# Projection and causal attention of layer 2 in one program

## What is computed

```python
h = rmsnorm(layernorm(x), ln1_w)
qkv = einsum('bsh,oh->bso', h, wqkv)     # 384 columns
q, k, v = 16 heads, 4 heads, 4 heads of 16 columns
q, k = apply_rope(q, cos, sin), apply_rope(k, cos, sin)
k, v = repeat(k, 4), repeat(v, 4)
scores = einsum('bqhd,bkhd->bhqk', q, k) * 16**-0.5   # causal mask
attn = einsum('bhqk,bkhd->bqhd', softmax(scores), v)
x = x + attn @ wo.T                       # then a mixture of experts
```

## Time and profile before

| | us |
|---|---|
| median of 3 runs | 2072.73 (2072.46 to 2073.15) |
| the profiled execution, its own time | 2073.89 |
| span of its trace | 2072.1 |
| PE busy | 1817.0 (88%) |
| DVE busy | 1227.2 (59%) |
| ACT busy | 990.4 (48%) |
| POOL busy | 504.0 (24%) |

### The profile page before, as it was taken

How to read it: one execution, slowest core, us unless ns; L and a number is a source line. 1 busy time by engine, 2 the same in 40 slices (tenths; PEclk the granted TensorE clock), 3 DMA queues, 4 the chain that set the end, 5 groups by cost and what they waited for, 6 DMA issues and landing times. The chain is left out here.

```text
span 2072.1 us, 33460 instructions
## 1 busy us (share of the span) xinstructions
PE 1817.0 (88%) x10357; PEld 958.4 (46%) x10358; DVE 1227.2 (59%) x3167; ACT 990.4 (48%) x2129; POOL 504.0 (24%) x740
## 2 busy tenths in 40 slices
PE   5795779884899999999999999999875799999994
PEld 5622656552333333333333333332665466666662
DVE  2388236886888888787888888782466122222220
ACT  2201115431477776767777776867643122222221
POOL 2100302366302030210203030000387122333331
PEclk9997899985899999999999999999986899999997
DMA  4000000000000000000000000000356222222223
GB/s 134 0 0 0 1 1 1 4 18 0 1 2 2 1 2 2 2 1 2 2 2 2 2 2 2 2 1 1 114 170 220 57 47 47 47 47 47 45 47 97
DMA packets 55929, 60.83 MB, mean 29 GB/s; under 512 B 11533, under 2 KB 51638, under 8 KB 55734
## 3 DMA queue, kind: packets, MB, share of 16 engines
q1 hardware_dynamic: 33712, 33.86, 5.5%
q0 software_dynamic: 13440, 18.36, 5.2%
q10 hardware_dynamic: 8646, 6.96, 1.0%
HBM read 34.82 MB, written 28.12 MB: 30 GB/s over the span
## 5 line engine op out<-in xcount | busy, mean ns | idle before, releaser
L1452 ACT ACTIVATE prob<-pS 128x512 f32<-128x512 f32 (+3 forms) x1280 | 600.3, 536 | 245.9 <-PE pS L1366 126.3
L1495 DVE TENSOR_REDUCE mx<-pM 128x1 f32<-128x512 f32 x768 | 501.2, 685 | 92.6 <-PE pM L1346 89.4
L1346 PE MATMUL pM<-KT,QT 96*128 96x512 bf16 (+3 forms) x1280 | 440.9, 356 | 11.7 <-ACT QT L1434 7.3
L1362 PE MATMUL pS<-QT,KT 99*128 99x512 bf16 (+3 forms) x1280 | 416.5, 350 | 14.5 <-ACT prob L1452 9.1
L1381 PE MATMUL pO<-prob,VV 128*32 128x512 f32 (+3 forms) x2560 | 300.6, 542 | 14.2 <-ACT prob L1452 14.0
L1491 DVE CUSTOM_DVE_ANT_0 junk<-pM,mask_row 128x128 bf16<-128x128 f32 (+3 forms) x512 | 243.6, 485 | 71.9 <-PE pM L1346 70.7
L2115 PE MATMUL pH<-w13T,QKV 128*128 x576 | 260.6, 595 | 1.7 <-ACT QKV L2161 1.7
L1346 PEld LDWEIGHTS pM<-KT,QT 96*128 96x128 bf16 x1280 | 124.0, 98 | 263.3 <-DVE mx L1495 99.6
L2203 DVE COPY QKV<-pG 128x512 f32<-128x512 f32 x72 | 49.8, 692 | 317.1 <-PE pG L2124 317.1
L1362 PEld LDWEIGHTS pS<-QT,KT 99*128 99x128 bf16 x1280 | 123.6, 98 | 148.8 <-ACT prob L1452 81.8
L1289 POOL CAST mpart<-mneg 128x16 bf16<-128x16 f32 x32 | 6.8, 213 | 749.6 <-DVE mneg L1503 749.6
(11 more groups left out here) (312 smaller groups left out, 2374.9 us busy)
## 6 DMA issues: line engine op xcount, KB each, us to landing
raw<-in_ffn_w_dram SPq DMA_DIRECT2D x48, 256.0 KB
QKV<-queue SPq DMA_DIRECT2D x72, 136.0 KB, 2.1
x<-_attn_hidden_states_dram SPq DMA_DIRECT2D x32, 128.0 KB, 2.2
acc<-x ACTq DMA_DIRECT2D x8, 512.0 KB
QT<-mrow SPq DMA_DIRECT2D x128, 3.0 KB
queue<-pad_rec SPq DMA_DIRECT2D x9, 136.0 KB
acc<-QKV POOLq DMA_INDIRECT x72
wc_s<-in_attn_Wc_dram ACTq DMA_DIRECT2D x1, 1024.0 KB
```

The lines of the kernel that those rows point to most:

```text
L1346: last = nc.tensor.matmul(pM[:, bank, 0:w], QT[0:ROWS, par, h, qt * P:(qt + 1) * P], KT[0:ROWS, par, 512 * part:512 * part + w], start=Tru ...
L1362: last = nc.tensor.matmul(pS[:, p % NSC, lo:512], KT[0:ROWS + 3, par, kt * P:(kt + 1) * P], QT[0:ROWS + 3, par, h, 512 * c + lo:512 * c + ...
L1452: nc.scalar.activation(prob[:, n % 3, h, lo:512], pS[:, p % NSC, lo:512], ACT.Exp, scale=SCALE).then_inc(s.head_exp, 1)
L1495: nc.vector.reduce_max(mx[:, h, qt, part:part + 1], pM[:, plan.bank[item], 0:w], AX.X).then_inc(s.unit_max, 1)
```

## The change

The two programs become one. The masks and fills are POOL's first instructions, the fill of KT among them. The first batch row (pairs 0 to 7) is projected as before, its rotations on DVE and POOL, eight each; all moments and roots come in this part, the last two groups after the rotations. Pairs 8 to 10 follow on PE and ACT, ahead of the first K and Q items; pairs 11 to 15 stand among the items of `plan.before`, one before every tenth or so. `plan.before` now reaches through the maxima of chunk 1 (65 items instead of 32), ahead of the first step. The second row's rotations are all on POOL, two tiles after the maxima of each of chunks 1 to 8. Buffers are shared: x transposed, the weights, DVE's products lie in `prob`, the transposes of x in `pO` (one buffer instead of two), the projections in the three banks of `pS` instead of four; each engine has one set of products instead of two.

```diff
-            stage5(nc, sb, ps, sem, locals(), v)
             stage6(nc, sb, ps, sem, locals(), v)
...
-    points = [(0.0, through[0])]
-    for k in range(1, CH * NG):
+    points = [(0.0, through[1])]
+    for k in range(2, CH * NG):
...
-    before = [x for x, d in zip(items, done) if d <= through[0]]
+    before = [x for x, d in zip(items, done) if d <= through[1]]
...
+        units = self.before[1 + GRP:]
+        self.front = [("P", i) for i in range(NP // 2, NP // 2 + 3)] + self.before[:1 + GRP]
+        late = [("P", i) for i in range(NP // 2 + 3, NP)]
+        for n, item in enumerate(units):
+            if late and n % (len(units) // (NP // 2 - 2)) == 0:
+                self.front.append(late.pop(0))
+            self.front.append(item)
...
+        def rotate(eng, ns, t, nth, byc, bys, by, turned):
+
+            eng.wait_ge(f.qkv_out, t + 1)
+            if nth:
+                eng.wait_ge(turned, nth)
...
+                pool.wait_ge(s.masks_b, 2)
+                nc.gpsimd.memset(KT[ROWS:ROWS + 3, :, :], 1.0).then_inc(s.ones_in, 1)
...
+                root(0)
+                root(1)
+                pool.wait_ge(f.small_in, 48)
+                for n in range(TB // 2):
+                    turn(2 * n + 1)
+                    if n % 2 == 0:
+                        root(n // 2 + 2)
+                root(6)
+                root(7)
+                pool.wait_ge(f.turned_dve, TB // 2)
+                pool.wait_ge(f.turned_pool, TB // 2)
...
                 prepare(0)
                 values_in(0)
+                later = list(range(TB, T))
                 for k in range(CH * NG):
                     maxima_parts(k)
...
+                    if k >= 1:
+                        for t in later[:2]:
+                            turn(t)
+                        del later[:2]
...
+                def projected_pair(i):
+                    if i + 1 < NP:
+                        turn(i + 1)
+                    project(i)
...
-                for item in plan.before:
-                    beside(item)
+                turn(0)
...
+                pe.wait_ge(f.wT_out, 12)
+                for i in range(NP // 2):
+                    projected_pair(i)
+                pe.wait_ge(s.masks_b, 2)
+                pe.wait_ge(s.ones_in, 1)
+                for item in plan.front:
+                    if item[0] == "P":
+                        projected_pair(item[1])
+                    else:
+                        beside(item)
+                pe.wait_ge(f.qkv_out, T)
+                pe.wait_ge(f.xT_out, NP)
                 pair(0, 0, lambda: None)
                 pair(0, 1, lambda: None)
...
-                nc.vector.memset(KT[ROWS:ROWS + 3, :, :], 1.0).then_inc(s.ones_in, 1)
...
+                for n in range(TB // 2):
+                    rotate(dve, nc.vector, 2 * n, n, byc_dve, bys_dve, f.by_dve, f.turned_dve)
+                    if n % 2 == 0:
+                        moments(n // 2 + 2)
+                moments(6)
+                moments(7)
+                dve.wait_ge(f.turned_dve, TB // 2)
+                dve.wait_ge(f.turned_pool, TB // 2)
```

More of the change, by code:

```diff
@@ L1441, in beside, with turned_out, projected, projected_pair @@
                         nc.scalar.copy(mrow[:, cols], pMb[bank][0:3 * GRP, 0:512]).then_inc(s.mrow_out, 1)
-                for item in plan.before:
-                    beside(item)
+                def turned_out(i):
+                    act.wait_ge(f.xT_mm, i + 1)
+                    if i >= 2:
+                        act.wait_ge(f.qkv_mm, 2 * i - 2)
+                    nc.scalar.copy(xT[:, i % 2], pT[:, :, :, :]).then_inc(f.xT_out, 1)
+                def projected(t):
+                    act.wait_ge(f.rms, t // G + 1)
+                    act.wait_ge(f.qkv_mm, t + 1)
+                    nc.scalar.activation(QKV[:, t, :], pS[:, t % NSC, 0:QKVW], ACT.Copy,
+                                         scale=rms[:, t:t + 1]).then_inc(f.qkv_out, 1)
+                def projected_pair(i):
+                    if i + 1 < NP:
+                        turned_out(i + 1)
+                    projected(2 * i)
+                    projected(2 * i + 1)
+                turned_out(0)
+                for i in range(NP // 2):
+                    projected_pair(i)
+                act.wait_ge(s.vv_init, 1)
+                for item in plan.front:
+                    if item[0] == "P":
+                        projected_pair(item[1])
+                    else:
+                        beside(item)
                 def exponential(n, h):
@@ L1466, in _, with moments @@
             def _(dve):
-                nc.vector.memset(KT[ROWS:ROWS + 3, :, :], 1.0).then_inc(s.ones_in, 1)
+                def moments(q):
+                    for t in range(G * q, G * q + G):
+                        nc.vector.bn_stats(stats[:, t, :], x1[:, t, :]).then_inc(f.stats, 1)
+                    for t in range(G * q, G * q + G):
+                        dve.wait_ge(f.stats, t + 1)
+                        nc.vector.bn_aggr(mv[:, t, :], stats[:, t, :]).then_inc(f.mv, 1)
+                moments(0)
@@ new lines, in _ @@
+                dve.wait_ge(f.ln_in, 16)
+                dve.wait_ge(f.raw_in, 48)
+                for n in range(3):
+                    nc.vector.tensor_tensor_reduce(scaled[:, n, :], raw[:, n, :], ln1_b, 1.0, 0.0, ALU.mult, ALU.add,
+                                                   wsum[:, 0, n:n + 1]).then_inc(f.w_times, 1)
+                dve.wait_ge(f.w_times, 3)
+                nc.vector.tensor_scalar(wsum[:, 1, :], wsum[:, 0, :], 1.0 / H, None, ALU.mult).then_inc(f.w_mean, 1)
+                dve.wait_ge(f.w_mean, 1)
@@ new lines, in _ @@
+                for n in range(3):
+                    nc.vector.tensor_scalar(scaled[:, n, :], scaled[:, n, :], wsum[:, 1, n:n + 1], None,
+                                            ALU.subtract).then_inc(f.w_ready, 1)
+                k = 0
+                for n in range(6):
+                    for c in range(C):
+                        dve.wait_ge(f.wT_mm, k + 1)
+                        rows = E if n == 5 else P
+                        dst = (wqkvT[:, c, n * P:(n + 1) * P] if n < 3 else v.woT[:, c, (n - 3) * P:(n - 2) * P]
+                               if n < 5 else v.gwT[:, c, :])
+                        nc.vector.tensor_copy(dst, pM[:, k % 2, 0:rows]).then_inc(f.wT_out, 1)
+                        k += 1
@@ L1471, in _ @@
-                split_queries(nc.vector, first, s.first_copied, 0, 0,
-                              [spare[:, r, 0:TB * GRP * HD].rearrange("p (t n) -> p t n", t=TB) for r in range(2)])
+                split_queries(nc.vector, first, s.first_copied, 0, 0, [rem[:, r] for r in range(2)])
                 dve.wait_ge(s.first_copied, 3)
+                assert first.k == 5
                 dve.wait_ge(s.qchain, 5)
```

267 lines of the change are left out of this document (93 added, 174 removed).

## The result

The changed kernel takes 2044.66 us (median of 4, 2043.53 to 2046.16) against 2072.60 of the kernel before (median of 4, three of them those of the table above): ratio 0.9869, 95% interval 0.9852 to 0.9886, a gain of 27.9 us. The profiled execution took 2046.16 for a span of 2044.3, 27.8 less than before.

What follows compares the result with a forecast made beforehand. VectorE's maxima bound 545 to 600, TensorE 600 to 1400; the win lies before 545. The second chunk's reduction 20.8 us earlier, less 2 given back, makes 18.8: from the median 2072.73 to 2053.9, range 2050 to 2058 (chance 0.52).

Steps and rivals of the forecast that it cites:

- The start: Projection start: PE's transposes of pair 1 ahead of the first projection add 1.0 us; POOL's early masks and fills stay hidden.
- One buffer instead of two: First row's rotations: each waits for the one before, 0.15 us seven times, 1.0 in all; eighth rotation ends at 463.7.
- The two roots: POOL's last two square roots, between the eighth rotation and the key split: 2.6 us with their gaps, until 466.3.
- The query split: VectorE's split of the queries from 463.8: 7.55 us, ready at 471.4, 0.6 us of slack against the key split.
- Keys at 472.0: Key split ready for PE's first transpose at 472.0, slightly after the queries; key and query transposes then end at 476.9.
- Pair 11: Second-row pair standing before the first unit on PE: 3.9 us, between full clock and 6 at half.
- First maximum: First maximum on VectorE at 481.1, against 505.74 in the kernel before.
- the pauses: VectorE starved by pairs 12 to 15 before the second chunk's reduction: 2.7 us four times, 10.8 (6.4 to 20).
- rival B: Attention start at full clock with short hand-offs, no single-buffer loss: pauses 6.4, gain 25 us, time 2048; chance 0.13.
- Given back: Step 0's scores and exponentials now follow the second chunk's maxima: 2 us of the gain lost (1 to 4).
- Moved into the loop: Second row's 16 rotations on POOL, 44 us after chunks 1 to 8, fit POOL's gaps and cost nothing.
- the unknowns upward: Slower side summed to 15 us: eighth rotation at 465, pair 11 and starvation at half clock, 4 given back.

Runs made afterwards that it cites:

- roots_later: Changed kernel with POOL's last two square roots moved behind the splits of keys and values; 2048.72 us, ratio 0.9879 to the kernel before.
- no_late_turns: Changed kernel with the second batch row's rotations (tiles 16 to 31) left out and not replaced; 2048.32 us, ratio 0.9881 to the kernel before.
- the twins: Kernel before and changed kernel, both unedited, run twice each on one chip: 2070.41 and 2070.86 us before, 2042.83 and 2047.38 us changed.
- pairs_first: Changed kernel with pairs 11 to 15 ahead of the key and query items instead of among the units; 2042.37 us, ratio 0.9845 to the kernel before.

## Why the prediction was wrong in size and right in kind

- **The start.** +1.0 was close: PE's first projection begins at 425.83 against 424.63, 1.2 later, of which 0.3 arose ahead of the layer. POOL's fill took 3.51 (forecast 3.8 between 0.95 and 3.8), hidden as said.
- **One buffer instead of two** was put at 1.0 and cost nothing visible. From the start of POOL's first rotation to the end of its eighth are 30.6 us (430.95 to 461.56), against the 32.4 that the forecast's terms make (31.9, plus 1.0, less 0.5). With a start 0.7 us later than before the eighth ends 2.1 us earlier than forecast. That fewer meetings with VectorE do this is argued from the shorter rotations, not tested.
- **The two roots**, 2.6, took 4.0 (461.56 to 465.57). Most of the excess is one instruction: line 1140 took 1.06 us at 463.41 and 0.19 at 461.64. The root ahead of it took 1.41 against 1.01. Both lie beside VectorE's query split, which begins at 461.66; roots_later shows the two at 2.7 where VectorE is idle. The forecast priced the roots from rows in which VectorE did something else. The key split took 5.8, forecast 5.7, and that was in part luck: its first two copies took 2.00 us for 0.75 before, its last cast 0.40 for 1.17, and in roots_later the whole of it took 7.4. The query split, priced at 7.55, took 6.4 and was ready 3.2 us before the keys, not 0.6.
- **Keys at 472.0**: 471.3, behind an idle TensorE from 460.31 on, as forecast (461). The errors cancelled in part. The two transposes were added up to 476.9 where 472.0, 1.06 and 3.62 make 476.7; they ended at 475.8. **Pair 11**: 3.9 forecast, 3.7 measured (475.60 to 479.33). **First maximum**: 481.1 forecast, 479.4 measured.
- **The failed step: the pauses.** I had 1.6 us a pair at full clock and 5 at half, and took 2.7 four times, 10.8, because a paced stretch had let the clock fall at 531. Measured are 1.90, 1.66, 2.13 and 1.26, together 6.95, with a granted clock of 1.00 from 482 to 510. This term is 3.9 us too large, and no other is so far off (the first maximum 1.7, the scores given back 0.7). The price of a pair at full clock was right and the weight between the two clocks wrong: the stretch at 531 had no dense fp32 block in it, and here there is one every ten units. What came true is nearest to rival B (full clock, short hand-offs, nothing lost to the single buffer), to which I gave 0.13: its 6.4 us of pauses were measured as 6.95, its 3.2 for pair 11 as 3.7. By the measured marks up to the router it is 25 us of gain, B's own sum. The full clock is not certain even so: in two of the five profiles of the changed kernel one pair of the four ran at half clock, and the pauses made 8.65.
- **Given back**: 2 forecast, 1.3 measured at the third chunk. **Moved into the loop**: nothing, as forecast; no_late_turns shows it. The Trainium skill's warning (Perfetto Trace Analysis, Optimizing Scalar/DVE Operations) agrees with the two roots beside the query split (1.06 against 0.19 us), though no run shows that the port is the cause. It does not show at the plain maxima, 685 ns with 32 us more of POOL's work beside them.
- **The range** ended 1.3 us above the result. By the phase alone, 25.4 to 26.4 us shorter, the time would be 2046.3 to 2047.3, just inside. The rest isn't the router's, which is equal on one chip. Counted from the layer's first transpose to the end, the twins differ by 27.4 us: 26.4 in the phase, 0.4 in the router stage, 0.6 behind it, from two profiles of each. Their times differ by 25.5 only (2070.64 less 2045.11), since the part ahead of the layer scatters: its first transpose comes at 407.1 to 413.1 in five profiles of the changed kernel, whose executions lie over 5 us apart. Of the medians' 27.9 and 28.2 that leaves less than 1 us without a place; whether the 1.0 behind the phase is the change's is open. Last, the unknowns upward, 15 us, would put the upper end at 2069, not 2067.

## What to carry to other kernels

A foreign block of work in an in-order queue costs its length less what is buffered behind it; cut it to pieces that the buffers cover, or put it where the queue waits anyway. Such a wait isn't quite empty room: work in it also keeps TensorE's clock up for what follows. In these runs the lower clock cost time where TensorE itself was waited for, and none under units that VectorE paced. When a serial step moves beside another engine's work, take its price from a row in which that neighbour is busy, and before a few microseconds are credited to a change, profile both kernels on the same chip, more than once.

## What the runs showed of the hardware

- TensorE's clock stayed at 1.00 from 482 to 510 in the changed kernel, dense fp32 pairs of 3.2 us alternating with units at VectorE's pace; in two more of the five profiles it did the same, and in two it was at half for one of the four pairs. Units without pairs ran at 0.50, before and in pairs_first.
- Behind a wait of 11.0 us the same transposes took 1.09 and 2.85 to 3.62 us that took 0.61 and 1.99 behind dense matmuls.
- The router stage took 157 us in seven of the profiles on two chips and in the changed kernel's first one, and 159 to 162 on two other chips and in the first profile of the kernel before, whatever the program ahead of it. The attention's tail took 44 or 46 us in one and the same program, as the granted clock stayed at 1.00 or fell to 0.50 for 6.8 us of it behind the same work.
- A small POOL instruction (128x4) beside VectorE's split took 1.06 us instead of 0.19, and both roots 4.0 instead of the 2.7 that they took where VectorE was idle; the same kind of key copies took 2.00 for two beside VectorE at 466.30, and 0.75 later in the loop:

```profile
616.32 0.75 POOL L1086 COPY Kt<-Kt 128x256 bf16<-128x256 bf16 x2 [0.17 <-POOL Kt L1084]
```
